# Upper key halves of the second sort brought to PSUM by ScalarE, one VectorE operand read from there

## What is computed

```
row, col = src, dst                       # messages go from x[col], pooled by row
messages = x[col]
gate = messages @ W_gate.T + b_gate       # one number per edge
h = messages @ W_lin.T + b_lin
e = exp(gate - segment_max(gate, row)[row])
attn = e / (segment_sum(e, row) + 1e-16)[row]
pooled = segment_sum(attn * h, row)
out = layernorm(x + pooled @ W_out.T + b_out)
```

## Time and profile before

| | |
|---|---|
| Time, median of 3 runs (range) | 2473.92 us (2473.26 to 2476.67) |
| The profiled execution: its time, its span | 2457.09 us, 2455.3 us |
| Busy share of the span: PE, DVE, ACT, POOL | 51%, 68%, 28%, 67% |
| Chain that ended last, by engine | POOL 55%, issue 20%, DVE 15%, PE 6% |
| First gather starts, last gather starts | 187.83 us, 2291.20 us |
| Gathers | 1661 |
| Mean granted TensorE clock | 0.635 of full speed |

### The profile page before, as it was taken

The page is one execution under the profiler, slowest core; times in us unless marked ns, Lnnn a source line. Parts: engine busy times, 40 slices in busy tenths (PEclk is TensorE's granted clock), DMA queues, the critical chain, the costliest instruction groups (busy, mean ns, idle before and its releaser), DMA issues.

```text
span 2455.3 us, 29482 instructions
## 1 busy us (share of the span) xinstructions
PE 1247.2 (51%) x5873; PEld 1070.4 (44%) x5873; DVE 1671.2 (68%) x6863; ACT 678.2 (28%) x2202; POOL 1644.2 (67%) x1708
## 2 busy tenths in 40 slices
PE   6810556544545445575665445443444345433776
PEld 4600445444444435464555334333443334433653
DVE  9997878877878875686667445554555446554787
ACT  3320233222322223203432223222322223221326
POOL 1007777777777777777777777777777777777205
PEclk9655555666565655666666566665666666666678
DMA  3023222222222222233222222222222222222333
GB/s 136 1 106 79 53 54 53 55 52 54 52 55 54 52 62 55 56 97 118 56 55 56 55 55 55 56 55 55 55 56 55 55 55 55 56 54 54 96 113 105
DMA packets 92096, 156.64 MB, mean 64 GB/s; under 512 B 29178, under 2 KB 61286, under 8 KB 91416
## 3 DMA queue, kind: packets, MB, share of 16 engines
q0 software_dynamic: 53152, 110.66, 20.1%
q1 hardware_dynamic: 38040, 43.90, 5.3%
q10 hardware_dynamic: 732, 0.20, 0.0%
HBM read 134.36 MB, written 20.28 MB: 63 GB/s over the span
## 4 chain that ended last, share of the span: by engine, by line
POOL 55%; issue 20%; DVE 15%; PE 6%; DVEq 1%; DMA 1%; ACT 0%; ACTq 0%; POOLq 0%; SPq 0%
POOL ring L578 55%; DVE nodes_sb L1246 4%; PE bank L911 4%; DVE first_keys L1128 3%; DVE first_keys L1129 3%; DVE spread L1241 1%; DMA ring<-node_table,gather_at 1%; PE bank L892 1%; DVE stats L1317 1%; PE bank L851 0%; DVEq L1235 0%; DMA ring<-in_dst 0%; DVE late_keys L1310 0%; PE bank L795 0%; ACTq L755 0%
## 5 line engine op out<-in xcount | busy, mean ns | idle before, releaser
L578 POOL DMA_INDIRECT ring<-node_table,gather_at x1661 | 1598.4, 962 | 673.7 <-issue 503.2
L911 PE MATMUL bank<-ring,spread 128*128 x3712 | 797.4, 393 | 358.3 <-DVE nodes_sb L1246 317.9
L911 PEld LDWEIGHTS bank<-ring,spread 128*128 128x128 f32 x3712 | 718.0, 293 | 416.5 <-issue 409.7
L1241 DVE TENSOR_SCALAR spread<-iota_row,places 128x128 f32<-128x128 f32 x1856 | 557.3, 301 | 326.1 <-PE bank L911 300.2
L1246 DVE SCALAR_TENSOR_TENSOR nodes_sb<-nodes_sb,drops,bank 128x130 f32 x1856 | 646.8, 349 | 4.4 <-issue 3.0
L680 ACT ACTIVATE ring<-ring,weights 128x129 f32<-128x129 f32 x1664 | 501.6, 391 | 3.6
L718 ACT ACTIVATE weights<-bank 128x40 f32<-128x40 f32 x42 | 8.5, 203 | 942.8 <-PE bank L873 942.8
L859 PE MATMUL bank<-ident,ring 128*40 128x128 f32 x42 | 16.2, 386 | 411.4 <-DMA ring<-node_table,gather_at 411.0
L1211 DVE TENSOR_TENSOR_SCAN run_max<-pen,bank 40x128 f32<-40x128 f32 x42 | 17.2, 409 | 304.9 <-PE bank L859 304.8
L859 PEld LDWEIGHTS bank<-ident,ring 128*40 128x40 f32 x42 | 5.2, 124 | 419.2 <-issue 419.2
L1128 DVE TENSOR_TENSOR late_keys<-late_keys 128x256 f32<-128x256 f32 x291 | 122.6, 421 | 6.5 <-ACT late_keys L638 3.5
(11 more groups left out here) (184 smaller groups left out, 1213.5 us busy)
## 6 DMA issues: line engine op xcount, KB each, us to landing
ring<-node_table,gather_at POOLq DMA_INDIRECT x1661
ring<-kept_sums SPq DMA_DIRECT2D x14, 455.0 KB, 5.5
node_table<-ring SPq DMA_DIRECT2D x1, 6347.7 KB
nodes_sb<-in_x SPq DMA_DIRECT2D x10, 625.0 KB
kept_sums<-nodes_sb SPq DMA_DIRECT2D x2, 2600.0 KB, 8.8
ring<-in_x SPq DMA_DIRECT2D x10, 448.0 KB, 6.4
out<-ring SPq DMA_DIRECT2D x10, 448.0 KB
k<-sorted_keys SPq DMA_DIRECT2D x126, 20.0 KB
```

The source lines that it names most:

```text
L578: pool.indirect_dma_start(out=chunk_rows[c % RING][:, t, :], out_offset=None, in_=table[:, :], in_offset=bass.IndirectOffsetOnAxis(ap=gath ...
L911: last = pe.matmul(tile_ps(slot), lhsT=spread[:, slot, :], rhs=ring[:, bass.ds(got[slot], ROW)], start=True, stop=True)
L1241: return dve.tensor_scalar(spread[:, slot, :], iota_row[:, :], places[r % 2][:, t:t + 1], None, ALU.is_equal)
```

## The change

Three things are changed; the number and the arithmetic of the exchanges stay.

1. **In-bank exchanges.** For 254 exchanges of the second sort (all `short` ones, `turned` and `rows` ones with `n > 0`, and those of `rows` with `k == 7`), ScalarE first copies the upper halves of the part, 256 columns, from SBUF to `turn_bank[g]` in PSUM (`copy_keys`). The copy waits for the part's step before. VectorE waits for the copy (`uppers_copied`), and reads the lower halves from SBUF and the upper halves from PSUM (`exchange_with_bank`).
2. **Exchanges behind a turn**, in both sorts: ScalarE copies only the upper halves out of the bank, and VectorE reads the lower ones from the bank (`exchange_turned`).
3. ScalarE's queue now goes through all steps of `late_order`, in which it went only through the turns.

```
+def in_bank(step):
+    h, g, k, kind, n = step
+    return h == 1 and (kind == "short" or kind in ("turned", "rows") and n > 0 or kind == "rows" and k == LOG_COLS)
...
+        def upper_keys(g, k, kind, n):
+            a, span = (turns if kind == "turned" else rows)[1][n % 2], span_of(k, kind, n)
+            cols = cols_of(1, g)
+            halves = a[:, cols].rearrange("p (a t j) -> p a t j", t=2, j=span)
+            return halves[:, :, 1, :], turn_bank[g][:, 0:(cols.stop - cols.start) // 2].rearrange("p (a j) -> p a j", j=span)
...
             def copy_turned(h, g, k, kind, n):
                 act.wait_ge(turned[h][g], turn_count(k, kind))
-                cols = cols_of(h, g)
-                into = (turns if kind == "forth" else rows)[h][0]
-                act.activation(into[:, cols], turn_bank[g][:, 0:cols.stop - cols.start], ACT.Copy).then_inc(turn_copied[h][g], 1)
+                upper = [halves_of(v, first_span(k, kind))[:, :, 1, :] for v in turned_keys(h, g, kind)]
+                act.activation(upper[1], upper[0], ACT.Copy).then_inc(turn_copied[h][g], 1)
+
+            late_done = [0, 0]
+
+            def copy_keys(h, g, k, kind, n):
+                if kind in ("forth", "back"):
+                    copy_turned(h, g, k, kind, n)
+                    return
+                if in_bank((h, g, k, kind, n)):
+                    act.wait_ge(*((steps_done[1][g], late_done[g]) if late_done[g] else (keys_built, 1)))
+                    upper, into = upper_keys(g, k, kind, n)
+                    act.activation(into, upper, ACT.Copy).then_inc(uppers_copied[g], 1)
+                late_done[g] += 1
+                if kind == "big" and 1 << k - LOG_BIG - 1 - n >= JOINT[1]:
+                    late_done[1] += 1
...
-                    for step in turnings(sort_slice(late_order, r, j)):
-                        copy_turned(*step)
+                    for step in sort_slice(late_order, r, j):
+                        copy_keys(*step)
...
+            def exchange_turned(h, g, b, k, kind):
+                dve.wait_ge(turn_copied[h][g], turn_count(k, kind))
+                in_bank, copied, vb = (halves_of(v, first_span(k, kind)) for v in turned_keys(h, g, kind) + (b[:, cols_of(h, g)],))
+                dve.tensor_tensor(vb[:, :, 0, :], in_bank[:, :, 0, :], copied[:, :, 1, :], ALU.min)
+                return dve.tensor_tensor(vb[:, :, 1, :], in_bank[:, :, 0, :], copied[:, :, 1, :], ALU.max)
+
+            uppers_used = [0, 0]
+
+            def exchange_with_bank(g, a, b, k, kind, n):
+                uppers_used[g] += 1
+                dve.wait_ge(uppers_copied[g], uppers_used[g])
+                _, upper = upper_keys(g, k, kind, n)
...
+                dve.tensor_tensor(vb[:, :, 0, :], lower, upper[:, :, ::-1] if mirrored else upper, ALU.min)
+                return dve.tensor_tensor(vb[:, :, 1, :], va[:, :, 0, ::-1] if mirrored else lower, upper, ALU.max)
```

More of the change, by code:

```diff
@@ L427, in turn_count, with first_span, halves_of, turned_keys @@
             return 2 * (k - LOG_COLS - 1) + (1 if kind == "forth" else 2)
+        def first_span(k, kind):
+            return 1 << (min(k - LOG_COLS, LOG_ROWS) if kind == "forth" else LOG_COLS) - 1
+        def halves_of(v, span):
+            return v.rearrange("p (a t j) -> p a t j", t=2, j=span)
+        def turned_keys(h, g, kind):
+            cols = cols_of(h, g)
+            return turn_bank[g][:, 0:cols.stop - cols.start], (turns if kind == "forth" else rows)[h][0][:, cols]
+        def upper_keys(g, k, kind, n):
[3 more added lines that the diff above has]
+            return halves[:, :, 1, :], turn_bank[g][:, 0:(cols.stop - cols.start) // 2].rearrange("p (a j) -> p a j", j=span)
         def table_upto(n):
@@ L707, in _ @@
             copy_prep(1)
-            for step in turnings(late_order[:FIRST_AHEAD]):
-                copy_turned(*step)
+            for step in late_order[:FIRST_AHEAD]:
+                copy_keys(*step)
             copy_prep(2)
-            for step in turnings(late_order[FIRST_AHEAD:SORT_AHEAD]):
-                copy_turned(*step)
+            for step in late_order[FIRST_AHEAD:SORT_AHEAD]:
+                copy_keys(*step)
             for r in range(ROUNDS):
@@ L1123, in exchange_mirrored @@
                 return dve.tensor_tensor(vb[:, :, 1, :], va[:, :, 0, ::-1], va[:, :, 1, :], ALU.max)
+            def exchange_turned(h, g, b, k, kind):
[8 more added lines that the diff above has]
+                _, upper = upper_keys(g, k, kind, n)
+                va, vb = (v[:, cols_of(1, g)].rearrange("p (a t j) -> p a t j", t=2, j=span_of(k, kind, n)) for v in (a, b))
+                lower = va[:, :, 0, :]
+                mirrored = SHORT[n][1] == SHORT[n][0] - 1 if kind == "short" else k == LOG_COLS and n == 0
+                dve.tensor_tensor(vb[:, :, 0, :], lower, upper[:, :, ::-1] if mirrored else upper, ALU.min)
+                return dve.tensor_tensor(vb[:, :, 1, :], va[:, :, 0, ::-1] if mirrored else lower, upper, ALU.max)
             def exchange(a, b, cols, span):
@@ L1173, in sort_step @@
                 elif kind == "turned":
-                    if n == 0:
-                        dve.wait_ge(turn_copied[h][g], turn_count(k, "forth"))
-                    ins = exchange(a, b, cols_of(h, g), 1 << min(k - LOG_COLS, LOG_ROWS) - 1 - n)
-                else:
-                    if n == 0 and k > LOG_COLS:
-                        dve.wait_ge(turn_copied[h][g], turn_count(k, "back"))
-                    ins = exchange_mirrored(h, g, a, b, k) if k == LOG_COLS and n == 0 else exchange(a, b, cols_of(h, g), 1 << LOG_COLS - 1 - n)
+                    ins = exchange_turned(h, g, b, k, "forth") if n == 0 else exchange(a, b, cols_of(h, g), 1 << min(k - LOG_COLS, LOG_ROWS) - 1 - n)
+                elif n == 0:
+                    ins = exchange_turned(h, g, b, k, "back") if k > LOG_COLS else exchange_mirrored(h, g, a, b, k)
+                else:
+                    ins = exchange(a, b, cols_of(h, g), 1 << LOG_COLS - 1 - n)
                 step_ends(h, g, ins)
```

14 lines of the change are left out of this document (12 added, 2 removed).

## The result

The changed kernel takes 2501.27 us (median of 4 runs, 2500.77 to 2505.79), the kernel before on the same chip 2473.59 us (2473.16 to 2476.67). The ratio of runs on record is 1.0126, with a 95% interval from 1.0092 to 1.016 (the two medians alone give 1.0112): slower, clear of the noise. The profiled execution took 2505.79 us, 48.7 us more than that of before (2457.09). The first gather starts at 189.86 us (before 187.83), the last at 2338.2 (before 2291.2), and the tail behind the last one is 165.8 us.

What follows compares the result with a forecast made beforehand. POOL's gather stream bounds the kernel; VectorE's copy waits, 92.4 us in twelve rounds, would make VectorE the pace to round 12, adding 46.4 us: 2503.5 us profiled, median 2520, range 2495 to 2558.

Steps and rivals of the forecast that it cites:

- (a): Slice 0, copy behind the weighing of batches 1 to 5: loss 2.5 us, or 1.75 with an exchange ahead; 21.0 us.
- (b): Slice 3, copy behind `copy_prep`, which waits for TensorE: loss 1.4 us in 10 rounds, 14.0 us.
- (c): Copy behind the turn of the other part in the same slice: 3.6 us in 9 cases, 32.4 us.
- (d): Copy in the slice behind a turn that held the other part's copy: 25 places at 0.5 us, 12.5 us.
- (e): Two exchanges of one part in a row: loss 0.57 us at 22 places not counted elsewhere, 12.5 us.
- The reserves hold: Rounds 0 to 12: with waits at 22 us or less POOL is the pace, full 24 us gained, 2450 us; chance 0.07.
- The lateness multiplies: Weighing behind a waiting copy delays TensorE's batch and VectorE's next step: 1 to 2 us a round more, 2540 us; chance 0.12.
- with the same difference the median goes from 2473.9 to 2520: Whole kernel: profiled execution forecast at 2503.5 us, with the earlier profile's 17 us under the median added again.

Runs made afterwards that it cites:

- early copies: Changed kernel with each in-bank copy issued right behind the step it waits for, ahead of turn copies, weighing, weights and copy_prep: 2439.06 us, ratio 0.991.
- the turns alone: Changed kernel without in-bank exchanges; only exchanges behind a turn read a bank, with turn copies halved: 2456.82 us, ratio 0.9984 to the kernel before.
- the waits alone: Changed kernel with copies, waits and queues kept, but VectorE reads both halves of in-bank exchanges from SBUF: 2500.71 us, ratio 1.0172 to the kernel before.

## Why the prediction was right, and where it was not

**What bounds it: right.** VectorE takes over the pace in rounds 0 to 12, the ring lets POOL start chunk 14 late, and behind that the gathers are back to their pace. POOL's wait for the ring was put at 60 to 70 us and was 68.0. Rounds of 55 to 57 us were forecast and 56.4 and 55.0 came.

**The sum: right.** Rounds 0 to 11 were to lose 92.4 us; they lost 932.7 - 267.0 - 577.3 = 88.4 (577.3 is 190.9 + 386.4 of the forecast). Round 12 starts at 932.7 (forecast 935.4), chunk 14 at 958.42 (forecast 960.8), and the profiled execution took 2505.79 against 2503.5. With early copies the same kernel falls to 2439 us, which shows that it is the places in the queue that cost, and not the copies as such.

**Its terms.** The forecast counted rounds 0 to 11. In these (a) was put at 21.0 and came to 20.2; (b) 14.0 and 14.1; (c) 32.4 and 34.8; (d) 12.5 and 12.5; (e) 12.5 and 13.8, at 22 places as counted. That (d) came out was luck: 25 places at 0.5 us were forecast, and it was 10 places at 1.25. The copy was mis-sized: 0.389 us instead of 0.50, so a copy that reads SBUF is priced like one that reads a bank (383 ns), and not by the line through L680. By itself this would have made the sum some 6 us too high (0.11 us at 60 waits, an estimate), but (c) and (e) came out 3.7 us above their forecast. In (a), 2.54 us less an exchange of 0.67 is 1.87 and not 1.75; the two places took 1.7.

**The exchange.** 416 and 413 ns against 420 with two SBUF operands. The Trainium skill's fixed term for PSUM (VectorE: DVE Perf Modes, section on the TRN2 errata), an estimated 65 ns more a half, is not borne out by it: here the half is 4 ns shorter, and the kernel that waits in the same way without the bank takes the same time.

**The rivals.** "The reserves hold" was rightly held unlikely in this queue order, and early copies show the condition that I gave for it: with 27.3 us of waits for copies instead of 105.0, and 22.5 of them in the twelve rounds, POOL is the pace. They ran in 2439 us where 2450 was worked out; that was 24 us off the upper level, and 24 off the lower would be 2434. "The lateness multiplies" is not seen: between 267.0 and 932.7 us VectorE waits 95.6 us for copies, and the twelve rounds are 88.4 longer, not more.

**The step that failed** is the last one, "with the same difference the median goes from 2473.9 to 2520". I took the 17 us between the profiled execution and the median for something that every kernel would carry. It belongs to kernels that POOL paces: in some executions of the kernel before one gather is shut out for the whole run of exchanges with two SBUF operands ahead of round 0. The four runs of the changed kernel lie on one level, at 2501 to 2506 us, 43 us above the lower level and 28 above the upper, and the median came at 2501.27 and not 2520.

The record gives two reasons. If a long gather came in the changed kernel, it would cost nothing. POOL stands still for longer at the first gather of chunk 5, for the ring:

```profile
461.95 0.94 POOL L606 DMA_INDIRECT ring<-node_table,gather_at  x1 [19.84 <-PE bank L952]
```

Nor would VectorE wait for gates by then, as chunks 0 to 4 have been gathered 25 to 44 us before they are turned. So the 15 us between the levels (2473.2 - 2457.9) are not lost again where VectorE is the pace, and I had added them. The four runs on one level thus can't tell whether the change also does away with the long gather.

For that there are the gathers that start 0.225 to 0.275 us behind the start of an exchange half with two or more halves close behind it. In the three profiles with exchanges from SBUF and without copies for them (two of the kernel before, and the turns alone) 14 of 34 such gathers take 1.3 us or more. In the changed kernel it is none of 11 and with early copies none of 8, and all of these took under 0.95 us. One of them starts at the head of the run ahead of round 0, 0.27 us behind the start of the first of 48 halves in a row:

```profile
218.50 0.40 DVE L1184 TENSOR_TENSOR late_keys<-late_keys,bank 128x256 f32<-128x256 f32 x1
218.77 0.94 POOL L606 DMA_INDIRECT ring<-node_table,gather_at  x1 [0.30 <-issue]
```

So with the bank operand no hold is seen. With copies and waits but both operands in SBUF holds are fewer, and they are still there: none of 7 such gathers with the waits alone, 2 of 12 in the three profiles with early copies, cut short at 2.0 us where a wait ends the run. That exchanges from SBUF are what holds a gather is shown by its length, too: 16.93 and 17.31 us for 24 steps, 9.26 for 12, 2.0 for two.

**Open.** What decides whether a gather that starts in those 0.05 us is held; how much rarer the waits alone make it; the share of the operand in the 19 us when the copies are early; why the first gather starts 2 us later (it lay between 186.2 and 190.1 us in the six profiles of 2440 to 2506 us, without an order that I could see); the 3.0 us from chunk 14 to the last gather and the longer tail; and the stops of VectorE on three chips.

## What to carry to other kernels

A helper copy on another engine is cheap by its duration and dear by its place: issue it as soon as its source is ready, ahead of everything in that queue that waits for a third engine. The same 254 copies at other places of the queue made 62 us of difference (2501.27 and 2439.06; 2500.71 on the same chip with the waits alone). And before a difference is added to a median, see whether the profiled execution and the median are on the same level; if they are not, find the row that makes the difference, as the change may touch it, or make another engine the pace so that it no longer counts.

## What the hardware showed that I had not expected

One indirect DMA issue on GpSimd took 16.93 and 17.31 us, and 9.26 us with half the exchanges, where its neighbours take about 1. It stayed shut out as long as VectorE ran tensor_tensor instructions with both operands in SBUF without a gap, and ended 1.4 us behind them each time. In another execution the gathers over the same exchanges took 1.04 us, and short holds of 1.3 to 2.7 us stand in the rounds of both levels. No gather was held by exchanges with an operand in a bank. The Trainium skill (SBUF — State Buffer, section Who interferes with whom) has such instructions contend with GpSimd where that reads SBUF; the rows agree in kind, with 0.04 to 0.09 us a gather as the usual price, and 16 us for one gather in the profiled execution of the upper level, on which 9 of 21 executions of the kernel before lie. And an ACTIVATE from SBUF to PSUM of 256 columns takes 389 ns, 6 ns more than one from PSUM to SBUF.
